# Moving work of the two bit-linear stages from VectorE and ScalarE to GpSimd: half of the normalising, most residual adds, and a shorter split into high and low parts

## The chip, the core and the metric

The kernel runs on one core of one Trainium2 chip. The metric is the device time of one execution in microseconds (us); the number that counts is the median of several runs. Engines are named as the profile names them: PE is TensorE, DVE is VectorE, ACT is ScalarE, POOL is GpSimd, SP is SyncE, which here only issues DMAs.

## The reference, cut to what matters

The network is a chain of six stages on 4 x 1024 rows of 256 features. The fourth and the sixth stage are the same "bit-linear" layer, and only they are touched:

```python
def _L1_ffn_ref(x, weight, ln_gamma, ln_beta):
    mu, var = mean(x), var(x)                              # over the 256 features
    xn = (x - mu) * rsqrt(var + 1e-3) * ln_gamma + ln_beta
    beta = mean(abs(weight))
    w_q = clip(round(weight / (beta + 1e-5)), -1, 1)
    gamma = max(abs(xn))                                   # over ALL rows
    xq = clip(xn * 128 / gamma, -128 + 1e-5, 128 - 1e-5)
    return (xq @ w_q) * (gamma * beta / 128)
...
x = x + 0.5 * _L1_ffn_ref(layernorm(x), ...)               # stage 4
x = x + _L1_attn_ref(layernorm(x), ...)                    # stage 5
x = x + 0.5 * _L1_ffn_ref(layernorm(x), ...)               # stage 6
```

The largest value over all rows splits the layer into two halves: nothing can be scaled before every row has been normalised.

## The kernel before, in words

The rows stay in SBUF for the whole kernel as `G.x`: 32 tiles of 128 rows by 256 features. `bit_phase` works on eight blocks (`NC`) of four tiles (`CT`). Each engine has its own program written out in order, and semaphores tie them together: `wait_ge` holds an engine, and everything queued behind on it, until a count is reached. A stage begins and ends with a barrier of all engines.

**First half.** For each block DVE normalises the four tiles (L1127, one `tensor_scalar` per tile with two per-row operands, written to `xn`, two buffers). PE transposes them into PSUM (`psT`, two buffers, L1197), ACT brings them to SBUF as `xT` with gain and bias (L1075), and DVE takes the largest absolute value (L1119, `largest(i-1)`, which stands behind `normalise(i)` on DVE). `normalise(i)` waits until the transposes of block i-2 are done. In between DVE sums the weights (L1106); GpSimd adds that over the partitions (L1061, `partition_all_reduce` to `wall`); DVE then makes the ternary weights (L1110 to L1114). At the end GpSimd takes the largest over the partitions (L1063, `gall`), and DVE works out `osc` and `gi` (L1138 to L1141).

**Second half.** ACT scales a block in place by `gi` (L1080), DVE clips it in place (L1145), ACT writes the fp16 high part `xhi` (L1085), DVE the fp16 rest `xlo` (L1152). PE multiplies both with the weights into `psY` (16 matmuls, L1208, two buffers). DVE adds the scaled result to the rows (L1158). In stage 4 DVE also takes the moments of the new rows for the next layernorm (L1166, L1172); in stage 6 SP sends each block out (L1054). `xhi`, `xlo` and `psY` have two buffers each, so block i waits for the matmuls (or the add) of block i-2.

Of the kernel before, what the change touches and what calls it, by code (L numbers as in the profile page):

```python
# [1004 lines left out]
def bit_phase(nc, G, A, r, out=None):  # L1005
# [3 lines left out]
    with ExitStack() as ctx:  # L1009
# [22 lines left out]
        xT = sb("xT", [P, NC, KD, CW])  # L1032
        xhi = sb("xhi", [P, 2, KD, CW], F16)
# [4 lines left out]
        s = sems(nc, ctx, f"bit{r}", "w_in gb_in eps sd norm var sd2 scl wsum wall quant xn xT xTev tmax max1 gmax gdve "  # L1038
                 "scaled xq xhi xlo Y out sums stat stored")
        block = ctx.enter_context(nc.Block())  # L1040

        @block.sync
        def _(sp):
# [6 lines left out]
            if last_phase:  # L1050
                rows = out.rearrange("b (t p) d -> p (b t) d", p=P)
                for i in range(NC):
                    sp.wait_ge(s["out"], ONE + i + 1)
                    sp.dma_start(rows[:, i * CT:(i + 1) * CT, :],  # L1054
                                 G.x[:, i * CT:(i + 1) * CT, :]).then_inc(s["stored"], 16)
# [3 lines left out]
        def _(pool):  # L1059
            pool.wait_ge(s["wsum"], ONE + 1)  # L1060
            nc.gpsimd.partition_all_reduce(wall[:, :], wsum[:, :], P, bass.bass_isa.ReduceOp.add).then_inc(s["wall"], 1)  # L1061
            pool.wait_ge(s["max1"], ONE + 1)
            nc.gpsimd.partition_all_reduce(gall[:, :], pmax[:, :], P, bass.bass_isa.ReduceOp.max).then_inc(s["gmax"], 1)  # L1063

        @block.scalar
        def _(act):
# [10 lines left out]
            act.wait_ge(s["gdve"], ONE + 4)  # L1077
            for i in range(NC + 1):
                if i < NC:
                    nc.scalar.activation(xT[:, i, :, :], xT[:, i, :, :], ACT.Copy, scale=gi[:, :]).then_inc(s["scaled"], 1)  # L1080
                if i >= 1:
                    act.wait_ge(s["xq"], ONE + i)
                    if i >= 3:
                        act.wait_ge(s["Y"], ONE + i - 2)
                    nc.scalar.activation(xhi[:, (i - 1) % 2, :, :], xT[:, i - 1, :, :], ACT.Copy).then_inc(s["xhi"], 1)  # L1085

        @block.vector
        def _(dve):
# [33 lines left out]
            for i in range(NC):  # L1122
                if i >= 2:
                    dve.wait_ge(s["xT"], ONE + (i - 1) * KD)
                for t in range(CT):
                    g = i * CT + t
                    nc.vector.tensor_scalar(xn[:, i % 2, t, :], G.x[:, g, :], G.mv[:, g, 0:1], scl[:, g:g + 1],  # L1127
                                            ALU.subtract, ALU.mult).then_inc(s["xn"], 1)
# [9 lines left out]
            step(dve, nc.vector.tensor_tensor(osc[:, :], gall[:, :], wall[:, :], ALU.mult), g)  # L1138
            step(dve, nc.vector.tensor_scalar(osc[:, :], osc[:, :], 0.5 / QB, None, ALU.mult), g)
# [1252 lines left out]
```

## Time and profile before

| | us |
|---|---|
| median of 3 runs (2425.19 to 2429.5) | 2425.92 |
| the profiled execution | 2436.6 |
| its span (first to last instruction) | 2434.7 |
| stage 4, first half (949.5 to 979.7 of the span) | 30.2 |
| stage 4, second half (979.7 to 1020.6) | 40.9 |
| stage 6, first half (2370.8 to 2401.0) | 30.2 |
| stage 6, second half (2401.0 to 2429.6) | 28.6 |
| last store and end (2429.6 to 2434.7) | 5.1 |
| busy over the span: PE 83%, DVE 66%, ACT 51%, POOL 20% | |

The two touched stages are 135 us of 2434.7, and the shares over the whole span say little about them. In the second half of stage 6 DVE is busy for 24.0 of 28.6 us, PE for 18.0, ACT for 16.7 and GpSimd not at all; in the first half of stage 4 DVE has 24.2 of 30.2 us. The stages have to be read one by one, in the timeline.

### The profile page before, as it was taken

How to read it: one execution, taken by the hardware profiler on the slowest of the kernel's cores; microseconds unless marked ns; L12 is line 12 of the kernel's file. 1: busy time of each engine (PE TensorE's matmuls, PEld its weight loads, DVE VectorE, ACT ScalarE, POOL GpSimd, SP SyncE). 2: the span in 40 equal slices, each digit the busy share in tenths (PEclk: the TensorE clock that was granted, in tenths of full speed). 3: DMA queues.
4: the chain of work that ended last, by engine and by line, in shares of the span. 5: the costliest groups of instructions: out<-in, count | busy, mean ns of one | idle time of the engine just before them, and what ended most of it. 6: DMA issues, size and time to landing. Idle time of an engine off the chain costs nothing. (4 is left out here: it accounts for less than half of the span.)

```text
span 2434.7 us, 74675 instructions
## 1 busy us (share of the span) xinstructions
PE 2030.2 (83%) x32204; PEld 1285.8 (53%) x32280; DVE 1617.5 (66%) x2553; ACT 1234.3 (51%) x1862; POOL 493.8 (20%) x794
## 2 busy tenths in 40 slices
PE   3986887888887796497773999999999999999975
PEld 2654555556455564354673555555555555555544
DVE  6775354453533677774353888888888888888847
ACT  3761221223212575322330677767777777777754
POOL 0002000000000000000001554444543454435410
PEclk7998999998989898698886899999999999999996
DMA  3001000000000000133237555544555455545412
GB/s 106 1 1 43 3 1 19 2 19 3 1 19 2 1 1 5 25 122 114 105 149 244 148 139 135 137 123 118 135 136 136 131 138 134 132 125 135 110 31 74
DMA packets 273793, 195.13 MB, mean 80 GB/s; under 512 B 206744, under 2 KB 260310, under 8 KB 273210
## 3 DMA queue, kind: packets, MB, share of 16 engines
q1 hardware_dynamic: 262586, 139.27, 22.5%
q0 software_dynamic: 10496, 50.75, 5.5%
q8 instruction: 256, 4.19, 0.7%
q14 instruction: 71, 0.58, 0.1%
q10 hardware_dynamic: 384, 0.33, 0.1%
HBM read 91.69 MB, written 93.88 MB: 76 GB/s over the span
## 5 line engine op out<-in xcount | busy, mean ns | idle before, releaser
L2020 DVE TENSOR_REDUCE a1c_nm<-a1c_S 128x1 f32<-128x1024 f32 x512 | 609.6, 1218 | 98.9 <-PE a1c_S L2105 98.3
L1960 ACT ACTIVATE a1c_PT<-a1c_ST 128x1024 f32<-128x1024 f32 x499 | 510.3, 1023 | 57.5 <-PE a1c_ST L2105 54.7
L1975 ACT ACTIVATE a1c_Pb<-a1c_S,a1c_nm 128x192 f32<-128x192 f32 (+1 forms) x512 | 212.9, 416 | 217.7 <-DVE a1c_nm L2020 216.7
L1904 POOL TENSOR_TENSOR a1c_lt<-a1c_lt 128x256 f32<-128x256 f32 (+5 forms) x448 | 254.7, 568 | 35.4
L2010 DVE COPY a1c_PbT<-a1c_T 96x512 f32<-96x512 f32 x256 | 175.7, 686 | 96.1 <-PE a1c_T L2137 93.7
L2105 PE MATMUL a1c_S<-a1c_KR,a1c_Q 54*32 54x512 f16 (+13 forms) x2816 | 180.7, 316 | 19.7 <-DMA a1c_Gx<-a_bias 18.3
L2105 PE MATMUL a1c_ST<-a1c_Q,a1c_KR 57*128 57x256 f16 (+2 forms) x1066 | 175.0, 284 | 22.3 <-ACT a1c_PT L1960 21.5
L2105 PE MATMUL a1c_S<-a1c_KL,a1c_Q 54*32 54x512 f16 (+11 forms) x3136 | 191.8, 323 | 0.6 <-ACT a1c_Pb L1975 0.3
L2105 PE MATMUL a1c_S<-a1c_Gx,ident 64*32 64x96 f32 (+2 forms) x4352 | 184.8, 240 | 0.0
L1896 POOL DMA_DIRECT2D a_band<-a1c_Pb x128 | 71.4, 558 | 495.6 <-ACT a1c_Pb L1975 495.3
L2137 PE MATMUL a1c_T<-ident,a1c_Pb 128*96 128x128 f32 x1024 | 168.1, 288 | 0.8 <-DVE a1c_mhl L2034 0.8
L2105 PE MATMUL a1c_ST<-a1c_Q,a1c_KL 57*128 57x128 f16 (+1 forms) x932 | 148.9, 265 | 19.2 <-ACT a1c_PT L1960 16.8
L1061 POOL PARTITION_ALL_REDUCE b_wall<-b_wsum x2 | 0.8, 406 | 799.1 <-DVE b_wsum L1106 799.1
L593 ACT ACTIVATE a_PT<-a_R 128x2048 f32<-128x2048 f32 x40 | 75.1, 1878 | 148.9 <-PE a_R L894 126.8
L2137 PEld LDWEIGHTS a1c_T<-ident,a1c_Pb 128*96 128x96 f32 x1024 | 101.9, 128 | 87.8 <-issue 55.4
L318 DVE TENSOR_TENSOR f_hlo<-f_h,f_hhi 128x512 f16<-128x512 f32 x128 | 88.0, 688 | 69.2 <-ACT f_hhi L236 69.2
L2105 PEld LDWEIGHTS a1c_S<-a1c_Gx,ident 64*32 64x32 f32 x4352 | 125.4, 109 | 13.6 <-issue 0.7
L231 ACT ACTIVATE f_h<-f_psH,b,a 128x512 f32<-128x512 f32 x128 | 99.3, 776 | 59.9 <-PE f_psH L342 58.4
L2105 PE MATMUL a1c_PV<-a1c_PT,a1c_VU 128*17 128x512 f32 (+3 forms) x1280 | 127.5, 470 | 0.0
L2105 PE MATMUL a1c_PV<-a1c_PT,a1c_VL 128*17 128x512 f32 (+3 forms) x1280 | 126.8, 468 | 0.2 <-issue 0.2
L1595 DVE TENSOR_TENSOR a1b_G<-a1b_k,a1b_G 128x512 f32<-128x512 f32 x96 | 65.7, 691 | 88.7 <-PE a1b_k L1601 49.5
L648 DVE TENSOR_REDUCE a_mt<-a_R 128x16 f32<-128x2048 f32 x32 | 73.4, 2293 | 75.0 <-PE a_R L835 75.0
(344 smaller groups left out, 4138.4 us busy)
## 6 DMA issues: line engine op xcount, KB each, us to landing
a_band<-a1c_Pb POOLq DMA_DIRECT2D x128, 384.0 KB, 3.3
a_bias<-a1b_G SPq DMA_DIRECT2D x32, 768.0 KB, 8.1
a1c_Gx<-a_bias SPq DMA_DIRECT2D x128, 192.0 KB, 4.3
a1c_Dt<-a_band SPq DMA_DIRECT2D x128, 126.0 KB, 3.7
a1c_Q<-a_qk SPq DMA_DIRECT2D x192, 64.0 KB
a1c_Vw<-a_values SPq DMA_DIRECT2D x64, 102.0 KB, 2.8
a1c_KL<-a_qk SPq DMA_DIRECT2D x96, 64.0 KB
a1c_KR<-a_qk SPq DMA_DIRECT2D x90, 64.0 KB
```

Source lines behind the costliest of these rows:

```text
L231: nc.scalar.activation(h[:, n % NB, :], psH[:, n % NB, :], ACT.Gelu, bias=G.b1[:, m:m + 1], scale=G.a1[:, m:m + 1]).then_inc(s["h"], 1)
L318: nc.vector.tensor_tensor(hlo[:, n % NB, :], h[:, n % NB, :], hhi[:, n % NB, :], ALU.subtract).then_inc(s["hlo"], 1)
L593: nc.scalar.activation(PT[:, n % 2, :, :], R[:, :, :], ACT.Exp, scale=0.25).then_inc(s["sexp"], 1)
L648: nc.vector.tensor_reduce(dst, src, AX.X, ALU.max, negate=True).then_inc(s["smax"], 1)
L1896: pool.dma_start(PW[b * S + I * P:b * S + I * P + P, 4 * hq:4 * hq + 4, :], Pb[:, at:at + 4, :]).then_inc(s[f"pw{g // 4 % 2}"], 16)
L1904: add = lambda o, x, y: nc.gpsimd.tensor_tensor(o, x, y, ALU.add)
L1960: nc.scalar.activation(PT[:, q % 8, :, :], place(q), ACT.Exp).then_inc(s["exp"], 1)
L1975: nc.scalar.activation(Pb[:, band_slot(I, c), w0:w1], SP[:, t % 2, I * P - 32 + w0:I * P - 32 + w1], ACT.Exp, bias=nm[:, t // 16 % 2, col: ...
L2010: nc.vector.tensor_copy(PbT[:, e % RING, :], T[0:BW, :]).then_inc(s["Tb_ev"], 1)
L2020: nc.vector.tensor_reduce(nm[:, t // 16 % 2, col:col + 1], SP[:, t % 2, :], AX.X, ALU.max, negate=True).then_inc(s["max"], 1)
L2105: return nc.tensor.matmul(out, w, x, start=start, stop=stop, skip_group_check=True)
L2137: ins = nc.tensor.transpose(T[0:BW, at:at + P], Pb[:, band_slot(I, c), BW * ch:BW * ch + BW], G.ident[:, :])
```

## The change

- First half: a helper `normalise` deals the tiles out. DVE takes tiles 0 and 2 of each block, GpSimd tiles 1 and 3, with a semaphore of its own (`xnp`). PE waits for both. GpSimd's all-reduce of the weight sum stands behind its tiles of block 1 and ahead of those of block 2.
- `gi` is worked out first; `osc` follows after the first block's low part.
- Second half: ACT writes `xhi` straight from `xT` with the scale `gi`. DVE scales and cuts at the upper bound into a new buffer `x1`, and cuts at the lower bound as it subtracts `xhi` (`scalar_tensor_tensor`). The step that scaled `xT` in place is gone.
- The scaled product goes from PSUM to a new buffer `ys` on ACT, and GpSimd adds it to the rows, for blocks 0 to 6. DVE does block 7 in one instruction, as before.

```diff
+        x1 = sb("x1", [P, 2, KD, CW])
+        ys = sb("ys", [P, 2, CT, D])
...
+        def normalise(eng, on, i, k, done):
+            for t in range(k, CT, 2):
+                g = i * CT + t
+                on.tensor_scalar(xn[:, i % 2, t, :], G.x[:, g, :], G.mv[:, g, 0:1], scl[:, g:g + 1],
+                                 ALU.subtract, ALU.mult).then_inc(done, 1)
...
         def _(pool):
+            pool.wait_ge(s["scl"], ONE + 2)
+            for i in range(NC):
+                if i >= 2:
+                    pool.wait_ge(s["xT"], ONE + (i - 1) * KD)
+                normalise(pool, nc.gpsimd, i, 1, s["xnp"])
+                if i == 1:
+                    pool.wait_ge(s["wsum"], ONE + 1)
+                    nc.gpsimd.partition_all_reduce(wall[:, :], wsum[:, :], P, bass.bass_isa.ReduceOp.add).then_inc(s["wall"], 1)
             pool.wait_ge(s["max1"], ONE + 1)
             nc.gpsimd.partition_all_reduce(gall[:, :], pmax[:, :], P, bass.bass_isa.ReduceOp.max).then_inc(s["gmax"], 1)
+            for i in range(NC - 1):
+                rows = G.x[:, i * CT:(i + 1) * CT, :]
+                pool.wait_ge(s["ys"], ONE + i + 1)
+                nc.gpsimd.tensor_tensor(rows, ys[:, i % 2, :, :], rows, ALU.add).then_inc(s["out"], 1)
...
-            act.wait_ge(s["gdve"], ONE + 4)
+            act.wait_ge(s["gdve"], ONE + 2)
             for i in range(NC + 1):
                 if i < NC:
-                    nc.scalar.activation(xT[:, i, :, :], xT[:, i, :, :], ACT.Copy, scale=gi[:, :]).then_inc(s["scaled"], 1)
-                if i >= 1:
-                    act.wait_ge(s["xq"], ONE + i)
-                    if i >= 3:
-                        act.wait_ge(s["Y"], ONE + i - 2)
-                    nc.scalar.activation(xhi[:, (i - 1) % 2, :, :], xT[:, i - 1, :, :], ACT.Copy).then_inc(s["xhi"], 1)
+                    if i >= 2:
+                        act.wait_ge(s["Y"], ONE + i - 1)
+                    nc.scalar.activation(xhi[:, i % 2, :, :], xT[:, i, :, :], ACT.Copy, scale=gi[:, :]).then_inc(s["xhi"], 1)
+                if i == 1:
+                    act.wait_ge(s["gdve"], ONE + 4)
+                if i >= 2:
+                    act.wait_ge(s["Y"], ONE + i - 1)
+                    if i >= 4:
+                        act.wait_ge(s["out"], ONE + i - 3)
+                    nc.scalar.activation(ys[:, i % 2, :, :], psY[:, i % 2, :, :], ACT.Copy, scale=osc[:, :]).then_inc(s["ys"], 1)
...
             def clip(i):
-                dve.wait_ge(s["scaled"], ONE + i + 1)
-                nc.vector.tensor_scalar(xT[:, i, :, :], xT[:, i, :, :], CLIP, -CLIP, ALU.min,
-                                        ALU.max).then_inc(s["xq"], 1)
+                if i >= 2:
+                    dve.wait_ge(s["xlo"], ONE + i - 1)
+                nc.vector.tensor_scalar(x1[:, i % 2, :, :], xT[:, i, :, :], gi[:, :], CLIP, ALU.mult,
+                                        ALU.min).then_inc(s["xq"], 1)
...
-                nc.vector.tensor_tensor(xlo[:, i % 2, :, :], xT[:, i, :, :], xhi[:, i % 2, :, :],
-                                        ALU.subtract).then_inc(s["xlo"], 1)
+                nc.vector.scalar_tensor_tensor(xlo[:, i % 2, :, :], x1[:, i % 2, :, :], -CLIP, xhi[:, i % 2, :, :],
+                                               ALU.max, ALU.subtract).then_inc(s["xlo"], 1)
...
             for i in range(NC):
-                pe.wait_ge(s["xn"], ONE + i * CT + CT)
+                pe.wait_ge(s["xn"], ONE + i * 2 + 2)
+                pe.wait_ge(s["xnp"], ONE + i * 2 + 2)
...
                 if i >= 2:
-                    pe.wait_ge(s["out"], ONE + i - 1)
+                    pe.wait_ge(s["ys"], ONE + i - 1)
```

The order of GpSimd's instructions in stage 4 before (L1058 begins its part; an ISA row without a tile is the change of library, one with a tile is an all-reduce):

```order
L1058 UNCONDITIONAL_BRANCH
L1061 ISA
L1061 ISA b_wall<-b_wsum 128x1
L1063 ISA b_gall<-b_pmax 128x1
L1009 UNCONDITIONAL_BRANCH
```

And the same place after the change (L1053 is the helper `normalise`, L1081 and L1083 the all-reduces, L1087 the adds):

```order
L1072 UNCONDITIONAL_BRANCH
L1053 ISA
L1053 TENSOR_SCALAR b_xn<-x,mv,b_scl 128x256 x4
L1081 ISA
L1081 ISA b_wall<-b_wsum 128x1
L1053 ISA
L1053 TENSOR_SCALAR b_xn<-x,mv,b_scl 128x256 x12
L1083 ISA
L1083 ISA b_gall<-b_pmax 128x1
L1087 ISA
L1087 TENSOR_TENSOR x<-b_ys,x 128x1024 x7
L1009 UNCONDITIONAL_BRANCH
```

Where there was one change of library there are five in stage 4; in stage 6 there are four, since the first one is missing there (the library is still loaded from stage 5).

DVE in the second half of stage 4 before, from `gi` on:

```order
L1141 TENSOR_SCALAR b_gi<-b_gi 128x1
L1145 TENSOR_SCALAR b_xT<-b_xT 128x1024 x2
L1152 TENSOR_TENSOR b_xlo<-b_xT,b_xhi 128x1024
L1145 TENSOR_SCALAR b_xT<-b_xT 128x1024
L1152 TENSOR_TENSOR b_xlo<-b_xT,b_xhi 128x1024
L1158 SCALAR_TENSOR_TENSOR x<-b_psY,b_osc,x 128x1024
L1145 TENSOR_SCALAR b_xT<-b_xT 128x1024
L1152 TENSOR_TENSOR b_xlo<-b_xT,b_xhi 128x1024
L1158 SCALAR_TENSOR_TENSOR x<-b_psY,b_osc,x 128x1024
L1166 BN_STATS b_sums<-x 128x6 x4
```

And after the change:

```order
L1164 TENSOR_SCALAR b_gi<-b_gi 128x1
L1169 TENSOR_SCALAR b_x<-b_xT,b_gi 128x1024
L1177 SCALAR_TENSOR_TENSOR b_xlo<-b_x,b_xhi 128x1024
L1181 TENSOR_TENSOR b_osc<-b_gall,b_wall 128x1
L1182 TENSOR_SCALAR b_osc<-b_osc 128x1
L1169 TENSOR_SCALAR b_x<-b_xT,b_gi 128x1024
L1177 SCALAR_TENSOR_TENSOR b_xlo<-b_x,b_xhi 128x1024
L1169 TENSOR_SCALAR b_x<-b_xT,b_gi 128x1024
L1177 SCALAR_TENSOR_TENSOR b_xlo<-b_x,b_xhi 128x1024
L1169 TENSOR_SCALAR b_x<-b_xT,b_gi 128x1024
L1177 SCALAR_TENSOR_TENSOR b_xlo<-b_x,b_xhi 128x1024
L1195 BN_STATS b_sums<-x 128x6 x4
```

The residual has left DVE's loop, and the low part of a block stands right behind its own cut, one block earlier in the loop than before.

## Rows read from the trace of the kernel before

**Rows 1.** Timeline: start us, us, engine, line, op [idle before <-releaser]; stage 4 opens.

```profile
953.04 2.67 DVE L1127 TENSOR_SCALAR b_xn<-x,mv,b_scl 128x256 f32<-128x256 f32 x8
...
956.45 0.41 POOL L1061 PARTITION_ALL_REDUCE b_wall<-b_wsum  x1 [755.63 <-DVE b_wsum L1106]
...
959.86 1.09 PE L1197 MATMUL b_psT<-ident,b_xn 128*128 128x128 f32 x8 [2.00 <-DVE b_xn L1127]
...
978.32 0.16 DVE L1135 TENSOR_REDUCE b_pmax<-b_tmax 128x1 f32<-128x8 f32 x1
...
979.75 2.19 ACT L1080 ACTIVATE b_xT<-b_xT,b_gi 128x1024 f32<-128x1024 f32 x2 [2.72 <-DVE b_gi L1141]
```

**Rows 2.** Timeline, stage 6, first half: where blocks 2 and 4 pass.

```profile
2381.18 1.97 PE L1197 MATMUL b_psT<-ident,b_xn 128*128 128x128 f32 x8 [1.71 <-DVE b_xn L1127]
...
2390.19 1.97 PE L1197 MATMUL b_psT<-ident,b_xn 128*128 128x128 f32 x8 [0.45 <-DVE b_xn L1127]
...
2393.01 1.22 DVE L1119 TENSOR_REDUCE b_tmax<-b_xT 128x1 f32<-128x1024 f32 x1
2394.14 1.37 DVE L1127 TENSOR_SCALAR b_xn<-x,mv,b_scl 128x256 f32<-128x256 f32 x4
...
2395.57 1.97 PE L1197 MATMUL b_psT<-ident,b_xn 128*128 128x128 f32 x8 [0.45 <-DVE b_xn L1127]
```

**Rows 3.** The chain that ended last, stage 6: start us, us, what.

```profile
2374.37 2.67 DVE b_xn L1127 x8
...
2401.08 2.19 ACT b_xT L1080 x2
...
2404.24 1.24 DVE b_xlo L1152
...
2405.61 3.58 PE b_psY L1208 x16
...
2426.36 1.94 PE b_psY L1208 x16
...
2428.32 1.28 DVE x L1158
```

**Rows 4.** Timeline of DVE, second half of stage 4, one block, and its last instruction.

```profile
995.36 1.25 DVE L1158 SCALAR_TENSOR_TENSOR x<-b_psY,b_osc,x 128x1024 f32<-128x1024 f32 x1
996.53 1.39 DVE L1166 BATCH_NORM_STATS2 b_sums<-x 128x6 f32<-128x256 f32 x4
...
999.85 1.25 DVE L1158 SCALAR_TENSOR_TENSOR x<-b_psY,b_osc,x 128x1024 f32<-128x1024 f32 x1
...
1020.17 0.38 DVE L1172 BATCH_NORM_AGGREGATE mv<-b_sums 128x2 f32<-128x6 f32 x4
```

**Rows 5.** Line L101, the kernel's first change of library: duration min/median/max ns, start us.

```profile
L101 POOLq MODIFY_POOL_CONFIG  x2: 11/11/11, 1.3 to 1.3; - x2
L101 POOL TENSOR_SCALAR_AFFINE_SELECT ident<-ident x1: 1239/1239/1239, 8.4 to 8.4; 128x128 f32<-128x128 f32 x1
```

**Rows 6.** Line L1061, the changes of library in both stages, same columns.

```profile
L1061 POOLq MODIFY_POOL_CONFIG  x4: 11/11/11, 949.7 to 2371.0; - x4
```

**Rows 7.** GpSimd's two-input instructions by form: busy us, mean ns.

```profile
L1904 POOL TENSOR_TENSOR a1c_lt<-a1c_lt 128x256 f32<-128x256 f32 x128 | 93.2, 728 | 10.0
L1920 POOL TENSOR_TENSOR a1c_VL<-a1c_VU,a_rvd 128x512 f32<-128x512 f32 x16 | 19.2, 1198 | 22.1 <-DMA a1c_VU<-a_values 21.8
L1926 POOL TENSOR_TENSOR x<-x,a1c_bp 128x2048 f32<-128x2048 f32 x4 | 18.2, 4547 | 0.1
```

**Rows 8.** Line L618, the same normalising on DVE at 183 to 198 us, GpSimd busy.

```profile
L618 DVE TENSOR_SCALAR a_xn<-x,mv,rstd x8: 1256/1316/5331, 183.6 to 196.1; 128x256 f32<-128x256 f32 x8
```

**Rows 9.** DVE instructions by form: busy us, mean ns.

```profile
L1127 DVE TENSOR_SCALAR b_xn<-x,mv,b_scl 128x256 f32<-128x256 f32 x64 | 21.8, 407 | 0.1
L1145 DVE TENSOR_SCALAR b_xT<-b_xT 128x1024 f32<-128x1024 f32 x16 | 11.0, 684 | 3.1 <-ACT b_xT L1080 3.1
L1152 DVE TENSOR_TENSOR b_xlo<-b_xT,b_xhi 128x1024 f16<-128x1024 f32 x16 | 19.5, 1219 | 0.8 <-ACT b_xhi L1085 0.8
```

More of the change, by code:

```diff
@@ L1037, in bit_phase, with wait_out @@
         psY = ps("psY", [P, 2, CT, D])
-        s = sems(nc, ctx, f"bit{r}", "w_in gb_in eps sd norm var sd2 scl wsum wall quant xn xT xTev tmax max1 gmax gdve "
-                 "scaled xq xhi xlo Y out sums stat stored")
+        s = sems(nc, ctx, f"bit{r}", "w_in gb_in eps sd norm var sd2 scl wsum wall quant xn xnp xT xTev tmax max1 gmax gdve "
+                 "xq xhi xlo Y ys out out_v sums stat stored")
         block = ctx.enter_context(nc.Block())
+        def wait_out(eng, i):
+            if i < NC - 1:
+                eng.wait_ge(s["out"], ONE + i + 1)
+            else:
+                eng.wait_ge(s["out_v"], ONE + 1)
+        def normalise(eng, on, i, k, done):
[3 more added lines that the diff above has]
+                                 ALU.subtract, ALU.mult).then_inc(done, 1)
         @block.sync
@@ L1124, in _ @@
                     dve.wait_ge(s["xT"], ONE + (i - 1) * KD)
[L1125 to L1128, printed above, removed]
+                normalise(dve, nc.vector, i, 0, s["xn"])
                 if i in (1, 3):
@@ L1151, in low_part, with out_scale, residual @@
                     dve.wait_ge(s["Y"], ONE + i - 1)
-                nc.vector.tensor_tensor(xlo[:, i % 2, :, :], xT[:, i, :, :], xhi[:, i % 2, :, :],
-                                        ALU.subtract).then_inc(s["xlo"], 1)
-            def residual(i):
-                rows = G.x[:, i * CT:(i + 1) * CT, :]
-                dve.wait_ge(s["Y"], ONE + i + 1)
-                nc.vector.scalar_tensor_tensor(rows, psY[:, i % 2, :, :], osc[:, :], rows, ALU.mult,
-                                               ALU.add).then_inc(s["out"], 1)
+                nc.vector.scalar_tensor_tensor(xlo[:, i % 2, :, :], x1[:, i % 2, :, :], -CLIP, xhi[:, i % 2, :, :],
+                                               ALU.max, ALU.subtract).then_inc(s["xlo"], 1)
+            def out_scale():
+                step(dve, nc.vector.tensor_tensor(osc[:, :], gall[:, :], wall[:, :], ALU.mult), g)
+                step(dve, nc.vector.tensor_scalar(osc[:, :], osc[:, :], 0.5 / QB, None, ALU.mult), g)
+            def residual():
+                rows = G.x[:, (NC - 1) * CT:, :]
+                dve.wait_ge(s["Y"], ONE + NC)
+                nc.vector.scalar_tensor_tensor(rows, psY[:, (NC - 1) % 2, :, :], osc[:, :], rows, ALU.mult,
+                                               ALU.add).then_inc(s["out_v"], 1)
             def moments(i):
-                dve.wait_ge(s["out"], ONE + i + 1)
+                wait_out(dve, i)
                 if i >= 1:
```

16 lines of the change are left out of this document (7 added, 9 removed).

## The prediction, made before the changed kernel was run

> **What bounds the kernel now.** The two touched stages are 135 us of 2434.7, so busy shares over the span say nothing; I read the timeline stage by stage, then the chain, then the costs of single lines. In the first half DVE is nearly always busy, yet the length is set by a ring. The transposes of one block start at 2390.19, ACT is done 2.8 later, DVE takes the largest (1.2, from 2393.01), then normalises the block after next (1.37), whose transposes start at 2395.57 [rows 2]. So two blocks cost 5.38. In the second half DVE sets the pace: cut 0.6, low part 1.15 and residual 1.2 make 2.93 per block in stage 6, and with the moments one block takes 4.49 in stage 4 (995.36 to 999.85 [rows 4]). The chain of stage 6 runs through `xlo`, the matmuls and the residual [rows 3]. GpSimd is idle there but for two all-reduces [rows 1].
>
> **First part of the change: GpSimd's order, with changes of library.** Every time GpSimd goes from all-reduce to ordinary arithmetic or back, the new order has a change of library. Its price is in the trace once, in the open: it is issued at 1.3 and the next instruction starts at 8.4, 7.1 us later, waiting for nothing else [rows 5]. A second row bounds it: issued at 949.7, the all-reduce starts at 956.45, just behind the weight sum it waits for, so the change was done within 6.7 [rows 6, 1]. Before, that one was hidden behind the start of the stage. I take 6.5, with 5.5 and 7.1 as ends, since one row allows less than 6.7; zero is a rival below. The skill says something here, and it does not carry the sum: "GPSIMD Engine Reference" of the Trainium skill, section 2.1 Instruction dispatch, has the first call after such a change pay about 6 us (5.95) for loading code. The 7.1 agrees in kind; by 5.95 the sum below would be some 4 us smaller.
>
> GpSimd's `tensor_scalar` on 128x256 has no row. Two inputs of that size take 0.73 [rows 7], DVE takes 0.34 to 0.41 for it [rows 2, 9]; I take 0.5, nearer the lower end because it reads one input, with 0.35 and 0.73 as ends.
>
> Stage 4: change issued at 949.7, done 956.2; four tiles (blocks 0 and 1), 958.2; change to all-reduce, 964.7; all-reduce 0.4, 965.1; change back, 971.6; two tiles of block 2, 972.6. The transposes of block 2 wait for that; they started at 959.86 [rows 1]: **+12.7**. DVE, PE and ACT all stand behind it, since DVE's next step needs that block. Stage 6: no change at the start; `scl` is ready at 2374.37 [rows 3], GpSimd gets the tiles once DVE's first four are through (see below), 2375.7; then 2377.7, 2384.2, 2384.6, 2391.1, 2392.1, against 2381.18 [rows 2]: **+10.9**.
>
> From there to the largest value took 18.6 (959.86 to 978.48 [rows 1]). After: the ring is shorter by half a normalising, 5.38 - 0.67 = 4.7; twice that for blocks 4 and 6, 2.0 until block 7, 2.8 + 1.2 + 0.2 for its end, 15.7: **-2.9** in each stage. The last change of library before the all-reduce of the largest is issued when block 7 is normalised, 5.3 to 6.0 ahead of the largest value by the same steps, so 0.5 to 1.2 of it stands out: **+0.7**. `gi` comes two small steps earlier: **-0.4**. The change ahead of the adds is hidden: the first add comes 8.9 after `gi`. Sum at `gi`: stage 4 12.7 - 2.9 + 0.7 - 0.4 = **+10.1**, stage 6 10.9 - 2.9 + 0.7 - 0.4 = **+8.3**.
>
> **Second part: the adds beside DVE.** A row shows that these two engines do not simply run side by side. DVE's `tensor_scalar` on 128x256 takes 0.41 [rows 9], but at 183 to 198, with GpSimd busy without a pause, eight of them took 1.26 to 5.33, median 1.32 [rows 8]. Each one waited for a whole GpSimd instruction. The new cut is such a `tensor_scalar` (SBUF to SBUF), so it excludes the add. For the low part, which reads two SBUF tiles, no row shows either; its cost from this lies between nothing and full exclusion. I take full exclusion, as the nearest row for an SBUF-to-SBUF step of DVE has it. Beside that stands a rule: "SBUF — State Buffer" of the Trainium skill, section Who interferes with whom, says that a DVE instruction with two SBUF inputs, or in its two-port mode, and a GpSimd instruction that reads SBUF lock each other out for a whole instruction. It speaks against this change; no run here shows the two-input half of it.
>
> GpSimd's add on 128x1024: 1.2 for 512 and 4.55 for 2048 elements [rows 7], 2.3 in between. Cut and low part keep 0.65 + 1.2 = 1.85 [rows 9, 3]. One block then costs 1.85 + 2.3 = **4.15** of the shared resource, against 2.93 in stage 6 and 4.49 in stage 4 before.
>
> From `gi` to the first add: high part 1.1, low part 1.2 (in place of the four steps to 2405.5, a gain of 2.1), 16 matmuls 3.5 at the 1.2 GHz that PE has at this point (3.58 against 1.94 later at 2.4 [rows 3]), high part of block 2 1.1, its low part and the next cut 1.85: 8.9 with the hand-overs. Stage 6: 8.9, four times 4.15, then add, low part, add, add = 2.3 + 1.2 + 2.3 + 2.3: 33.6. Before, 2401.04 to 2429.60 = 28.6 [rows 3]: **+5.0**. The residual of block 7 on DVE and its matmuls finish earlier than the last add, so they cost nothing; if the adds were quick, they would be the end. Stage 4: seven adds 16.2; the moments (1.4, one input) run beside an add and let a second add pass, so only about four cut-and-low pairs stand between them, 7.5; with 8.9 the last add ends at 32.6; low part 7, four rounds of moments and the residual follow on DVE, 9.4: 42.0. Before, 979.71 to 1020.55 = 40.8 [rows 1, 4]: **+1.2**. ACT's new evacuation (1.1) and high part (1.1) make 2.2 per block, hidden under 4.15; uncovered it would set 2.2. Stores follow the adds on SP, and the tail of 5.1 stays.
>
> **Sum**: 10.1 + 8.3 + 5.0 + 1.2 = 24.6, **+25 us**. The profiled execution would go from 2436.6 to about 2461; the median of the runs is 10.7 lower than the profiled one, 2425.9 + 25 = **2451**. Laid out in this way with the old steps, the ends of both stages come within 0.3 us of the trace's.
>
> **Rivals.** (1) *Reload paid, but only the cut and the normalising exclude GpSimd, the low part does not.* Then a block costs 0.65 + 2.3 = 3.0 in stage 6, and stage 4 falls back to DVE's own 3.5: 8.5 less, +16, 2442. For it: no row has a two-input step blocked. Against: none has it free.
> (2) *Reload paid, no exclusion at all.* GpSimd's 2.3 per block is the pace of stage 6, 3.5 on DVE that of stage 4; the second halves gain 4 and 8, and the first halves lose the 18 less 2 for waits: about +4, 2430. Against: rows 8.
> (3) *The other side: changing the library costs nothing on the path*, for instance because a library seen once stays. The place is GpSimd's tiles of block 2. First halves then gain 3.9 each (three rings 2.0, the start 1.5, `gi` 0.4), and with no exclusion the second halves gain 8 and 4: -20, 2406. With exclusion the normalising takes turns too, which leaves 1.7 in each first half: against the 6.2 of the second halves +3, 2429, or, with the cut alone excluding, second halves of 6.2 - 8.5 and -6, 2420. The sign turns, without exclusion, where a change costs 5.8; with the cut alone excluded, at 3.3; with full exclusion it does not turn. For it: nothing says that a library loaded before must be loaded again. Against: rows 5 and the fact that the order has a change each time.
> (4) *Changing costs more than 7.1 each, or the first instruction after one is slow* (the first after rows 5 took 1.24): each further us costs 7 in all, +30 or more.
>
> **How the numbers follow.** Forecast 0.56, its own range 2446 to 2460: changes of 5.5 to 7.1 give +20 to +30, tiles of 0.35 to 0.73 -3 to +4. Rival 1 0.17, rival 2 0.09, rival 3 0.12 (0.05 without exclusion, 0.02 with the cut alone, 0.05 in full), rival 4 0.06. The range **2428 to 2462** takes in the forecast, rival 1, most of rival 2 and the full-exclusion case of rival 3, and leaves out some 0.17. A measurement here can tell about 0.2%, 4.9 us, from no change. Faster by more: the two cases of rival 3, 0.07. Within: half of rival 2 and the case of +3, 0.10. Slower: 0.83.
>
> **What would show it.** Right: in both stages GpSimd's first tile of block 2 starts about 6.5 after the all-reduce of the weight sum, with nothing it waits for, and PE's transposes of block 2 at about 973 and 2392; `gi` at about 990 and 2409; cuts and low parts of DVE that last 3 us or start only when an add ends; adds 4.15 apart in stage 6. Wrong: block 2's transposes before 962, adds of 2.3 beside low parts of 1.2 (rivals 1 and 2), or a second half of stage 6 shorter than 28. If PE stayed at 1.2 GHz through the second half, a block would need 3.5 there, still hidden under 4.15. What would make it wrong altogether is a library change that runs ahead while GpSimd waits.

## The result

The changed kernel takes **2471.4 us** (median of four runs, 2467.4 to 2475.6) against 2427.7 for the kernel before (2425.2 to 2431.5): a ratio of 1.0179, with an interval of 1.0155 to 1.0203. It is slower by 43.7 us, where 25 were forecast, and lies 9 us above the top of the range. The profiled execution took 2469.6 us, its span is 2467.9.

The profile of after says where. I cut both stages as the prediction did: the first half runs from the stage's first instruction on DVE to the first one that uses `gi`, the second to the last instruction that writes `x`, the tail to the end of the span.

| us | stages 1 to 3 | 4, first | 4, second | stage 5 | 6, first | 6, second | tail | the two stages |
|---|---|---|---|---|---|---|---|---|
| before | 949.5 | 30.2 | 40.8 | 1350.3 | 30.2 | 28.5 | 5.1 | 134.9 |
| after | 942.1 | 43.2 | 43.8 | 1353.7 | 43.8 | 34.7 | 6.6 | 172.1 |
| forecast | | 40.3 | 42.0 | | 38.5 | 33.6 | 5.1 | 159.5 |

The two stages that were changed grew by 37.2: 26.6 in the first halves, 9.2 in the second, 1.5 in the tail.

**First halves.** GpSimd in stage 6, from its timeline (start us, us, engine, line, op, idle before and what ended it):

```profile
2386.33 5.03 POOL L1053 TENSOR_SCALAR b_xn<-x,mv,b_scl 128x256 f32<-128x256 f32 x4 [39.97 <-DVE b_scl L1127]
2397.17 0.40 POOL L1081 PARTITION_ALL_REDUCE b_wall<-b_wsum  x1 [5.82 <-issue]
2405.03 14.82 POOL L1053 TENSOR_SCALAR b_xn<-x,mv,b_scl 128x256 f32<-128x256 f32 x12 [7.46 <-issue]
2425.76 0.38 POOL L1083 PARTITION_ALL_REDUCE b_gall<-b_pmax  x1 [5.91 <-issue]
2435.11 2.44 POOL L1087 TENSOR_TENSOR x<-b_ys,x 128x1024 f32<-128x1024 f32 x1 [8.97 <-ACT b_ys L1113]
```

Every passage from the tiles to an all-reduce or back has 5.8 to 7.5 us of "issue" ahead of it: GpSimd waits for nothing that the profile shows. These are the changes of library. GpSimd waits for nothing else until `gi`: from the stage's start 3.6 to its first tile, then 5.0 + 5.8 + 0.4 + 7.5 + 14.8 + 5.9 + 0.4, and 0.4 on DVE for `gi` make the 43.8, and in stage 4 the same steps make the 43.2. So GpSimd's own work is the path through the whole first half, with 19.9 of tiles and 19.2 of changes (stage 6). The profile's chain, below, goes by the other engines' steps there and has 1.6 of issue left over behind the largest value; GpSimd's steps leave nothing over. The second thing to see is the length of the tiles: four of them 5.03. The line by itself (duration min/median/max in ns, first and last start) has both engines side by side:

```profile
L1053 DVE TENSOR_SCALAR b_xn<-x,mv,b_scl x32: 401/407/636, 945.6 to 2418.7; 128x256 f32<-128x256 f32 x32
L1053 POOL TENSOR_SCALAR b_xn<-x,mv,b_scl x32: 1208/1216/1408, 945.7 to 2418.6; 128x256 f32<-128x256 f32 x32
```

The same instruction takes 0.41 on DVE and 1.22 on GpSimd; the forecast had 0.5. DVE's stay short even where a tile of GpSimd runs beside them (24 of the 32 do so, the longest took 0.64), so here neither engine waits out the other's instruction. Everybody stands behind block 2, as the timeline of stage 6 shows, with PE's transposes of blocks 1 and 2 and DVE's first largest value after them:

```profile
2391.50 1.94 PE L1228 MATMUL b_psT<-ident,b_xn 128*128 128x128 f32 x8 [0.46 <-POOL b_xn L1053]
...
2407.58 1.94 PE L1228 MATMUL b_psT<-ident,b_xn 128*128 128x128 f32 x8 [14.14 <-issue]
...
2410.37 1.22 DVE L1147 TENSOR_REDUCE b_tmax<-b_xT 128x1 f32<-128x1024 f32 x1 [10.92 <-ACT b_xT L1099]
```

In [rows 2] those transposes come 10.35 after the stage's start at 2370.8, here 24.9 after 2382.7.

In stage 4 the all-reduces have the same 5.67 and 5.84 ahead of them and the tiles of block 2 6.95, but ahead of the first tiles, at 945.69, no time is lost to a change:

```profile
945.69 5.03 POOL L1053 TENSOR_SCALAR b_xn<-x,mv,b_scl 128x256 f32<-128x256 f32 x4 [745.27 <-DVE b_scl L1127]
956.39 0.40 POOL L1081 PARTITION_ALL_REDUCE b_wall<-b_wsum  x1 [5.67 <-issue]
963.74 14.89 POOL L1053 TENSOR_SCALAR b_xn<-x,mv,b_scl 128x256 f32<-128x256 f32 x12 [6.95 <-issue]
984.48 0.38 POOL L1083 PARTITION_ALL_REDUCE b_gall<-b_pmax  x1 [5.84 <-issue]
```

**Second halves.** DVE in stage 6, five steps of its timeline:

```profile
2434.10 1.23 DVE L1177 SCALAR_TENSOR_TENSOR b_xlo<-b_x,b_xhi 128x1024 f16<-128x1024 f32 x1 [2.09 <-ACT b_xhi L1106]
2435.24 2.85 DVE L1169 TENSOR_SCALAR b_x<-b_xT,b_gi 128x1024 f32<-128x1024 f32 x1
2438.13 3.25 DVE L1177 SCALAR_TENSOR_TENSOR b_xlo<-b_x,b_xhi 128x1024 f16<-128x1024 f32 x1
2441.30 2.83 DVE L1169 TENSOR_SCALAR b_x<-b_xT,b_gi 128x1024 f32<-128x1024 f32 x1
2444.16 1.23 DVE L1177 SCALAR_TENSOR_TENSOR b_xlo<-b_x,b_xhi 128x1024 f16<-128x1024 f32 x1
```

A cut takes 0.75 when it is alone and 2.85 beside an add, a low part 1.23 and 3.25. The excess is 2.0 to 2.1, just under the 2.35 of an add: the instruction waits out the rest of the add that is running. The adds wait in the same way, with 2.34 at the least and 3.33 at the most:

```profile
L1087 POOL TENSOR_TENSOR x<-b_ys,x x14: 2344/2458/3328, 993.6 to 2458.3; 128x1024 f32<-128x1024 f32 x14
```

The chain that ended last runs through these steps (start us, us, what):

```profile
2424.16 1.60 issue
2425.76 0.39 POOL b_gall L1083
...
2429.19 3.59 PE b_psY L1239 x16
...
2438.13 3.26 DVE b_xlo L1177
2441.39 0.05 issue
2441.43 3.47 PE b_psY L1239 x16
...
2456.23 1.24 DVE b_xlo L1177
2457.46 0.05 issue
2457.51 2.49 PE b_psY L1239 x16
2460.00 0.03 issue
2460.02 1.28 DVE x L1187
```

It shows both kinds of price: 1.6 of issue between the largest value and its all-reduce, and low parts of 3.26. It shows a third thing as well. The matmuls that follow a long low part, after 4.1 in which PE stood idle, take 3.47 for a block, against 1.94 in [rows 3]. The granted clock there is 0.53, so nearly all of it ran at the lower level of 1.2 GHz, where before's block of 1.94 had 1.00 (2.4 GHz):

```profile
2441.40:2445.00 3.60, 3.46 (x16) 2.17 (x16) 3.56 (x2) 0.07 (x1) 2.18 (x1) 0.53 0.54 182
2426.60:2461.30 34.70, 21.48 (x128) 15.07 (x128) 29.18 (x19) 15.94 (x15) 18.99 (x7) 0.73 0.27 92
```

The columns are the stretch, us, the busy times of PE, weight loads, DVE, ACT and GpSimd, then clock, DMA share and GB/s. Over the whole second half, the second line, the clock is 0.73 of full speed, where before's second half of stage 6 had 0.82.

### The profile page after: what moved, and what is told of

Read it like the earlier page. It is cut to its first block and busy times, and to the rows that moved or that the text cites. A ratio compares the mean times of both kernels' runs of the same rounds, so it can differ in the third digit from the quotient of the medians.

```text
span 2467.9 us, 74775 instructions
## 1 busy us (share of the span) xinstructions
PE 2045.2 (83%) x32280; PEld 1284.4 (52%) x32280; DVE 1615.6 (65%) x2507; ACT 1232.1 (50%) x1860; POOL 568.0 (23%) x840
## 5 line engine op out<-in xcount | busy, mean ns | idle before, releaser
L1935 POOL TENSOR_TENSOR a1c_lt<-a1c_lt 128x256 f32<-128x256 f32 (+5 forms) x448 | 253.9, 567 | 35.4
L1053 POOL TENSOR_SCALAR b_xn<-x,mv,b_scl 128x256 f32<-128x256 f32 x32 | 39.7, 1250 | 799.7 <-DVE b_scl L1127 785.2
```

Of the source, the lines that this page charges most:

```text
L1935: add = lambda o, x, y: nc.gpsimd.tensor_tensor(o, x, y, ALU.add)
```

## The experiments

The theory after the result: the first halves pay for changes of library and for GpSimd tiles of 1.22, the second halves for DVE and GpSimd shutting each other out in cut and low part. Against it stood that one half's loss might come from the other (a clock, a late `x`), that changes cost less than they seem and only the slow tiles count, and that low parts are long for another reason than the adds. The runs are read by the table of stages, since a profile shows a stage to some tenths of a us while whole runs of one kernel differ by 5 and more. All stages in us; medians where a kernel was timed in rounds, with their ratio to before on the same chip.

| | 4, first | 4, second | 6, first | 6, second | tail | the two stages | against before |
|---|---|---|---|---|---|---|---|
| before | 30.2 | 40.8 | 30.2 | 28.5 | 5.1 | 134.9 | 1 |
| after | 43.2 | 43.8 | 43.8 | 34.7 | 6.6 | 172.1 | 1.0179 |
| adds alone | 29.9 | 43.6 | 29.7 | 34.4 | 7.0 | 144.6 | 1.0047 |
| tiles alone | 43.6 | 40.8 | 43.6 | 28.5 | 5.7 | 162.2 | 1.0119 |
| all-reduces last | 30.1 | 46.8 | 30.9 | 37.5 | 5.7 | 151.0 | 1.0103 |
| one tile | 38.1 | 47.4 | 38.1 | 36.0 | 5.7 | 165.3 | one run |
| two changes, in before | 36.4 | 41.4 | 36.3 | 28.5 | 5.7 | 148.3 | one run |
| scratch adds, in before | 30.2 | 52.1 | 30.2 | 41.2 | 5.7 | 159.4 | one run |
| scratch memsets, in before | 30.2 | 44.4 | 30.2 | 35.4 | 5.7 | 146.0 | one run |
| short split | 29.9 | 40.4 | 29.9 | 26.9 | 5.1 | 132.1 | 0.9996 |
| short split, a tile on ACT | 28.0 | 40.4 | 28.0 | 26.8 | 5.1 | 128.3 | 0.9972 |

### The two parts apart

**Adds alone** is the changed kernel with its first half as before: DVE normalises every tile, GpSimd has only the all-reduces there.

```diff
-            for t in range(k, CT, 2):
+            for t in range(CT):
...
-            pool.wait_ge(s["scl"], ONE + 2)
-            for i in range(NC):
-                ...
-                normalise(pool, nc.gpsimd, i, 1, s["xnp"])
...
+            pool.wait_ge(s["wsum"], ONE + 1)
+            nc.gpsimd.partition_all_reduce(wall[:, :], wsum[:, :], P, bass.bass_isa.ReduceOp.add).then_inc(s["wall"], 1)
```

> First half of both stages as in the kernel before (DVE normalises every tile), second half as in the changed kernel (GpSimd adds, ACT's scaled copy, short split). Theory (library changes and GpSimd's slow tiles cost the first halves 26 us, mutual exclusion of DVE and GpSimd the second halves 9 and the tail 1.5): first halves back to 30 us each, second halves 43 to 44 and 34 to 35, total 9 to 12 above before. Rival (what was lost in the second halves comes from their late start, with PE at 1.2 GHz after the long idle time): the second halves too fall back to 41 or less and 29 or less, total within 3 of before or faster.

Measured: 2446.55 against 2430.4, ratio 1.0047 (1.0022 to 1.0072). The first halves are those of before to 0.6, the second ones those of after to 0.3.

**Tiles alone** is the kernel before with the changed first half:

```diff
+                normalise(pool, nc.gpsimd, i, 1, s["xnp"])
+                if i == 1:
...
...
-                for t in range(CT):
-                    nc.vector.tensor_scalar(xn[:, i % 2, t, :], ...)
+                normalise(dve, nc.vector, i, 0, s["xn"])
```

> First half as in the changed kernel (GpSimd normalises tiles 1 and 3), second half as before (DVE cuts and adds everything). Theory: first halves 43 to 44 us each in place of 30, second halves 41 and 28.6 as before, total 25 to 29 above before. Rival (the parts are not independent, the adds' library change is what makes the first half long): first halves under 38, total under +16.

Measured: 2459.01, ratio 1.0119 (1.008 to 1.0158), first halves 43.6, second halves as before. Over before the two stages grew by 9.7 and by 27.3; together that is 37.0, and the whole change has 37.2. So the parts add up, and neither half's loss comes from the other. The adds alone also carry the longer tail (7.0): the last add on GpSimd and DVE's residual end 0.2 us apart there (2439.7 and 2439.9), so that two stores are left for the end.

### How much of the first halves is library, how much the tiles

**All-reduces last** is the changed kernel with both all-reduces behind GpSimd's last tile, so that one change of library is left in the first half; the ternary weights follow behind DVE's first low part.

```diff
                 normalise(pool, nc.gpsimd, i, 1, s["xnp"])
-                if i == 1:
-                    pool.wait_ge(s["wsum"], ONE + 1)
-                    nc.gpsimd.partition_all_reduce(wall[:, :], ...)
+            pool.wait_ge(s["wsum"], ONE + 1)
+            nc.gpsimd.partition_all_reduce(wall[:, :], ...)
             pool.wait_ge(s["max1"], ONE + 1)
...
-                if i in (1, 3):
-                    quantise(i // 2)
+                if i == 1:
+                    quantise(0)
...
                 if i == 0:
+                    quantise(1)
                     out_scale()
```

> The changed kernel, but the all-reduce of the weight sum stands next to that of the largest value at the end of GpSimd's first half, and the ternary weights are made after the first block's low part. That removes two changes of library from the middle of each first half and puts 1.75 us of DVE work and 0.4 of all-reduce later. Theory (each change costs 5.7 to 7.4 on the path): first halves 43 to about 31, the second ones up to 2 longer, total 18 to 24 below the changed kernel. Rival (GpSimd's tiles of 1.22 us are what makes the first half long, the changes are mostly hidden): at most 8 below the changed kernel.

Measured: 2456.34, ratio 1.0103 (1.0066 to 1.0139). The two stages are 21.2 below after: the first halves fall from 43.2 and 43.8 to 30.1 and 30.9, and the second ones, with the weights in them now, grow by 3.0 and 2.7. GpSimd in stage 6:

```profile
2381.81 19.74 POOL L1053 TENSOR_SCALAR b_xn<-x,mv,b_scl 128x256 f32<-128x256 f32 x16 [40.00 <-DVE b_scl L1126]
2407.91 0.40 POOL L1080 PARTITION_ALL_REDUCE b_wall<-b_wsum  x1 [6.35 <-issue]
2408.23 0.44 POOL L1082 PARTITION_ALL_REDUCE b_gall<-b_pmax  x1
```

Sixteen tiles take 19.74, two per block 2.47, and the transposes of one block follow those of the last in 2.44. The chain that ended last runs through them:

```profile
2381.81 1.39 POOL b_xn L1053
2383.21 18.35 POOL b_xn L1053 x15
...
2401.80 6.11 issue
2407.91 0.40 POOL b_wall L1080
```

So GpSimd's tiles and one change of library are the whole path of this first half, and that it is as long as before's is a coincidence. From block 2's transposes to the largest value it takes 16.4 in place of 18.6, by the shorter normalising; but those transposes start 0.9 later, and 1.6 to 2.4 of the change stand out behind the largest value. Halving DVE's normalising gained nothing, because GpSimd's tiles of 1.22 became the pace.

**One tile** leaves one tile of four to GpSimd and three to DVE:

```diff
-            for t in range(k, CT, 2):
+            for t in ((3,) if k else (0, 1, 2)):
```

> The changed kernel with GpSimd normalising one tile per block (3) in place of two, DVE three. Theory (a GpSimd tile of 1.22 us ahead of each change of library lengthens the path: two tiles fewer before the first change, one fewer before block 2's transposes): each first half 3.5 shorter than in the changed kernel, about 40, less 0.5 for DVE's longer ring: 40 to 41. Rival (the tiles are hidden, only the changes count): 43 to 44 as before.

Measured: first halves of 38.1, 5.1 and 5.7 below after. More than expected, and the trace says why. Three tiles instead of six stand ahead of block 2, 3 x 1.22 = 3.7, and its transposes come 3.4 and 4.1 earlier. From there to the largest value it takes 0.6 less. And GpSimd is done early enough that its all-reduce comes 0.5 after the largest value in place of 1.6, so that the profile has it waiting for that value again:

```profile
987.34 0.38 POOL L1083 PARTITION_ALL_REDUCE b_gall<-b_pmax  x1 [5.91 <-DVE b_pmax L1160]
```

The second halves brought a surprise. Their code is that of after, and stage 4's took 47.4, not 43.8 (one execution of each). Low parts of stage 4 on DVE in both kernels, after first (busy us, mean ns):

```profile
L1177 DVE SCALAR_TENSOR_TENSOR b_xlo<-b_x,b_xhi 128x1024 f16<-128x1024 f32 x8 | 11.8, 1478 | 2.6 <-ACT b_xhi L1106 2.4
```

```profile
L1177 DVE SCALAR_TENSOR_TENSOR b_xlo<-b_x,b_xhi 128x1024 f16<-128x1024 f32 x8 | 15.9, 1983 | 2.8 <-ACT b_xhi L1106 2.6
```

4.1 us more in which low parts wait for adds: three of the eight are long in place of one. That this depends on where the steps happen to fall is my reading; what is measured is that the length of such a stage differs by some us for the same code.

### What one change of library costs

**Two changes** puts a GpSimd instruction of no use to the result (128x1 elements) between the largest value and its all-reduce, in the kernel before:

```diff
             pool.wait_ge(s["max1"], ONE + 1)
+            nc.gpsimd.tensor_scalar(tiny[:, :], pmax[:, :], 0.5, None, ALU.mult).then_inc(s["tiny"], 1)
+            pool.wait_ge(s["tiny"], ONE + 1)
             nc.gpsimd.partition_all_reduce(gall[:, :], ...)
```

> The kernel before, with one GpSimd multiplication of 128x1 between the largest value over the blocks and the all-reduce of it, so that a change of library and the change back stand on the path and nothing else is added. Theory: about 7.2 and 5.8, each first half 13 longer (43), total +26. Rival (a change of library is cheap when no data moves besides, or a library that was loaded once is kept): under +4 in all.

Measured: +6.2 and +6.1 in the first halves, half of what was expected, and so a miss that tells more than a hit. Stage 4:

```profile
956.49 0.40 POOL L1062 PARTITION_ALL_REDUCE b_wall<-b_wsum  x1 [755.71 <-DVE b_wsum L1109]
978.63 0.27 POOL L1064 TENSOR_SCALAR b_tiny<-b_pmax 128x1 f32<-128x1 f32 x1 [21.73 <-DVE b_pmax L1138]
984.79 0.38 POOL L1066 PARTITION_ALL_REDUCE b_gall<-b_pmax  x1 [5.89 <-issue]
```

The change toward arithmetic was asked for just behind the first all-reduce, which ends at 956.90, and ran while GpSimd waited for the largest value; the small instruction starts as soon as that is there. Here is the change's own row (min/median/max ns, first and last start us):

```profile
L1064 POOLq MODIFY_POOL_CONFIG  x4: 83/83/83, 956.9 to 2390.3; - x4
```

Only the change back is in the open, 5.89 and in stage 6 5.77. So a change doesn't begin when the wait ahead of its instruction ends but when the instruction before it is done. It is hidden by any wait as long as itself, and in the changed kernel nothing like it stands ahead of the tiles of block 2: there is 5.8 + 7.5 with no wait between.

A change can also cost nothing at all. In before, the first instruction behind the change at L101 starts 7.1 later [rows 5]; in after it starts at once (1.46 to 1.52):

```profile
L101 POOLq MODIFY_POOL_CONFIG  x2: 11/11/11, 1.4 to 1.5; - x2
L101 POOL TENSOR_SCALAR_AFFINE_SELECT ident<-ident x1: 292/292/292, 1.5 to 1.5; 128x128 f32<-128x128 f32 x1
```

The eleven profiles divide without exception: at once in the five kernels whose last change is the one toward arithmetic for adds, 6.8 to 7.7 later in the six whose last change is the one toward an all-reduce. That reads as a library that stays loaded from one execution to the next, and as a change that is free when its library is already there. Stages 1 to 3 show no gain from it (941 to 950 us in the five, 938 to 950 in the six).

### Who shuts whom out

Both kernels are the one before, with work for GpSimd on a scratch tile beside its second halves; it is extra work, and so only the length of DVE's instructions and of the halves is read. **Scratch adds** has two memsets and then seven adds of 128x1024 in each stage, **scratch memsets** ten memsets of 128x2560, each about as long as an add (2.2 to 2.7) but writing only.

```diff
+            nc.gpsimd.memset(scr[:, 0, :], 0.0)
+            nc.gpsimd.memset(scr[:, 1, :], 0.0)
+            for i in range(7):
+                nc.gpsimd.tensor_tensor(scr[:, 2, 0:1024], scr[:, 0, 0:1024], scr[:, 1, 0:1024], ALU.add)
```

```diff
+            for i in range(10):
+                nc.gpsimd.memset(scr[:, i % 3, :], 0.0)
```

> The kernel before, with seven GpSimd adds of 128x1024 on tiles of their own, which nobody waits for, beside the second half of each stage. Theory (DVE and GpSimd exclude each other for a whole instruction if DVE works SBUF to SBUF in its fast form, or reads two SBUF tiles): while the adds run, the cut and also the low part last up to 3 us in place of 0.68 and 1.22, the residual (one input from PSUM) stays at 1.28; the second halves grow by 5 to 10 each. Rival 1 (only the cut is excluded): low parts stay at 1.22, growth 3 to 5. Rival 2 (the long instructions of the changed kernel came from its data flow): nothing grows by more than 0.5.

> The same with ten GpSimd memsets of 128x2560 (about 2.3 us each), which read nothing. Theory: the cut waits for whole memsets, the low part (two reads, one write) does not and stays at 1.22. Rival (any GpSimd instruction excludes any SBUF-only DVE instruction): low parts last up to 3 us as in the run with adds.

DVE beside the adds: cut, low part, residual (min/median/max ns).

```profile
L1152 DVE TENSOR_SCALAR b_xT<-b_xT x16: 670/1644/2827, 972.5 to 2441.9; 128x1024 f32<-128x1024 f32 x16
```

```profile
L1159 DVE TENSOR_TENSOR b_xlo<-b_xT,b_xhi x16: 1201/1224/3371, 976.5 to 2444.8; 128x1024 f16<-128x1024 f32 x16
```

```profile
L1165 DVE SCALAR_TENSOR_TENSOR x<-b_psY,b_osc,x x16: 1244/1272/1285, 981.5 to 2448.0; 128x1024 f32<-128x1024 f32 x16
```

And beside the memsets, the first two of them:

```profile
L1149 DVE TENSOR_SCALAR b_xT<-b_xT x16: 670/1540/2757, 978.5 to 2436.8; 128x1024 f32<-128x1024 f32 x16
```

```profile
L1156 DVE TENSOR_TENSOR b_xlo<-b_xT,b_xhi x16: 1203/1206/1218, 981.8 to 2439.7; 128x1024 f16<-128x1024 f32 x16
```

Here the steps of DVE share no tile with GpSimd's work and wait for none of its results, and they are as long as in after. So it is the engine beside them, not the kernel's own order. The cut, which in one read and one write goes from SBUF to SBUF (0.67 for 1024 elements), is held up by both kinds; the low part, which reads two tiles of SBUF, by the reading add alone (up to 3.37) and never by the memset (1.22 at most, though ten of the sixteen run beside one); the residual, one of whose two tiles is in PSUM, by neither (1.29 at most). "SBUF — State Buffer" of the Trainium skill, section Who interferes with whom, has just this: two SBUF inputs against a GpSimd instruction that reads SBUF, and the two-port mode against any. The two traces agree with the first, and with the second if the cut runs in that mode, which no row names. That section has the one engine blocked for the other's whole instruction; the cuts and low parts show this, the normalising of the first half doesn't, with 0.23 lost at most.

The second halves grew by 11.3 and 12.7 beside the adds, where 5 to 10 were expected; two memsets of 2.3 ahead of the adds are part of it, and how the rest adds up I did not follow.

### Is there a gain in it at all

**Short split** keeps what is good in the new second half (ACT writes the high part straight from `xT`, DVE clips and scales in one) and gives GpSimd nothing; DVE adds every residual between cut and low part.

```diff
-            for i in range(NC - 1):
-                pool.wait_ge(s["ys"], ONE + i + 1)
-                nc.gpsimd.tensor_tensor(rows, ys[:, i % 2, :, :], rows, ALU.add).then_inc(s["out"], 1)
...
                     clip(i)
+                if 2 <= i <= NC + 1:
+                    residual(i - 2)
+                if i < NC:
                     low_part(i)
```

> No work on GpSimd beyond the two all-reduces: ACT writes the high part straight from xT with the scale, DVE scales and cuts into x1 and takes the low part, and DVE adds every block from PSUM. Theory: DVE's pace per block stays 3.0 and 4.5, the start of each second half is 2.1 us shorter and gi comes 0.4 earlier, cuts with a pointer cost 0.07 each more: 4 us faster than before. Rival (DVE is bound everywhere, the start is paid back at the end): within 1 us of before. Rival (the ring through the high part's wait on the matmuls binds with two buffers): up to 5 slower.

Measured: 2428.54 against 2430.4, ratio 0.9996 (0.9979 to 1.0012), the two stages 2.8 shorter, 1.6 of it at the second half of stage 6 and 0.4 at that of stage 4. No difference that a run can tell. DVE is the pace of these halves, and the new cut costs it as much as the old one or more; here is the new one, to be read against the 684 of [rows 9]:

```profile
L1148 DVE TENSOR_SCALAR b_x<-b_xT,b_gi x16: 734/746/753, 968.0 to 2413.1; 128x1024 f32<-128x1024 f32 x16
```

**Short split with a tile on ACT** then tries the idea of the first half with an engine that has neither a library to change nor a quarrel with DVE: ACT normalises the fourth tile of each block, `x * scl + nb` with `nb` = -mean x `scl` from one small instruction of DVE.

```diff
+            def own_tile(i):
+                nc.scalar.activation(xn[:, i % 2, CT - 1, :], G.x[:, g, :], ACT.Identity, bias=nb[:, g:g + 1],
+                                     scale=scl[:, g:g + 1]).then_inc(s["xna"], 1)
...
-            for t in range(CT):
+            for t in range(CT - 1):
```

> The short split without GpSimd, and ACT normalises tile 3 of each block (an activation with scale and bias per row, right behind its evacuations), DVE three tiles. Theory (the first half is set by the ring transposes, evacuation, largest value, normalising on DVE): each ring of two blocks 0.34 shorter, first halves about 28.7 in place of 29.9, total 5 below the kernel before (0.2%). Rival (ACT's extra 0.5 per block delays the evacuations): first halves 30 or more, total as with the short split alone.

Measured: 2425.61 (12 runs) against 2435.2 (16) on the same chip, ratio 0.9972 (0.9952 to 0.9992). It beats the kernel before by 0.3%, by more than the runs' uncertainty though not by much, and the changed kernel by far. The first halves are 2.2 shorter. ACT takes 0.59 for a tile and DVE's own stay at 0.41, so neither is held up by the other:

```profile
L1084 ACT ACTIVATE b_xn<-x,b_nb,b_scl x16: 585/591/600, 950.7 to 2385.6; 128x256 f32<-128x256 f32 x16
```

```profile
L1050 DVE TENSOR_SCALAR b_xn<-x,mv,b_scl x48: 402/405/409, 950.6 to 2387.5; 128x256 f32<-128x256 f32 x48
```

## Why the prediction was right or wrong

**The mechanisms held.** Both of the forecast's are in the traces: a change of library in the open on the path to block 2, once each way, and full exclusion of cut and low part. For the low part the exclusion was a choice between two ends that no row decided, and it came true. It was taken for the normalising too, and there it failed: DVE's tiles beside GpSimd's took 0.41 with 0.64 at most. The 1.26 to 5.33 of [rows 8] were measured beside other GpSimd instructions, memsets and selections of 0.9 to 1.2; what makes the difference stays open. Rival 1 (low part free) falls by low parts of 3.25 in after and 3.37 beside scratch adds, rival 2 with it. Rival 3 (changes free) falls by 5.8 and 7.5 of issue and by the 21.2 that come back when the all-reduces go last. "A library change that runs ahead while GpSimd waits", named as what would make it wrong altogether, does exist (two changes in before, one of them hidden). Rival 4 had the range in which the time fell (+30 or more), for another reason: the first instruction after a change took 1.41 at most, and the changes themselves are near the forecast's. The sum itself had let two changes run ahead in this way, the one before the largest value and the one before the adds. The hidden change didn't overturn the forecast, because ahead of block 2 there is no wait to hide in.

**The size did not.** The two stages grew by 37.2, not 24.6:

- *The tile on GpSimd, 0.5 with ends 0.35 and 0.73: measured 1.22.* This is the step that failed. It was bounded from above by an add of the same size [rows 7] on the thought that one input is cheaper than two. But this `tensor_scalar` takes two more operands, a mean and a scale for each row, and no row of GpSimd had that form; whether these are what makes it slow, no run tells. Six tiles ahead of block 2 make 6 x 0.72 = 4.3 in each stage, 8.6 in all. The instruction stood in [rows 9] on DVE alone, and a bound above would have had to come from rows further off. It also turned the path around: the forecast let the ring of PE, ACT and DVE set the pace behind block 2, and in the trace GpSimd goes from tile to tile without a wait and sets it.
- *Change of library, 6.5 each.* 5.8 toward the all-reduce and 7.5 toward arithmetic in stage 6: 13.3 for 13.0, a good term. The 5.95 of "GPSIMD Engine Reference" of the Trainium skill (section 2.1 Instruction dispatch) is met toward the all-reduce and exceeded by up to 1.5 the other way. In stage 4 the first of three (ending at 956.2 in the forecast) did not stand out: the tiles start 3.6 after the stage's start, in step with `scl`. That took off 3.1. The library that GpSimd used last, 745 us earlier, was one of ordinary arithmetic, so that there was probably nothing to load. The two ways the kernel starts, shown under the experiment with two changes, support this.
- *Wait of 1.3 for DVE's first tiles in stage 6*: not there. Tiles on GpSimd and DVE started within 0.1 of each other and ran side by side, -1.3. The whole for block 2 is then 14.5 in stage 6 (10.9 forecast) and 13.9 in stage 4 (12.7).
- *Ring shorter by 2.9*: 16.6 from block 2's transposes to the largest value against 18.6 before, so 2.0; +0.9 in each stage. The blocks follow each other in 2.4 to 2.5, which is GpSimd's two tiles.
- *Last change before the largest value, 0.7*: 1.6 in the chain, +0.9 in each. It is asked for when GpSimd's last tile is done, and that comes later by the slow tiles: the same error again. With one tile per block it was 0.5.
- *Second half of stage 6, 33.6*: 34.7. The first add came 8.6 after `gi` (8.9). From there to the end of the last add it was 25.5 (24.7 forecast), of which GpSimd is busy 19.0 and waits 6.6 for ACT and, through it, for PE and the low part. Matmuls of 3.5 at 1.2 GHz were to be hidden under the 4.15 of a block; here they stand in the chain behind a low part of 3.26. Then the residual of block 7, which was to be done earlier, ends 0.6 behind the last add, its matmuls having taken 2.5 where they take 1.94 at full clock.
- *Second half of stage 4, 42.0*: 43.8. Given 43.6 to 47.4 for the same code in other kernels, this isn't a number that could be had closer.
- *The tail stays 5.1*: 6.6. Since add 6 and residual 7 end within 0.7 us of each other, their stores go out together. In adds alone they end 0.2 apart and the tail is 7.0; in the nine other kernels they end 2.1 or more apart, and it is 5.1 to 5.7.

First halves +8.2, second halves +2.9, tail +1.5: 12.6 more than the sum. The price of the tile makes 12.2 of the first halves' (8.6, 1.8 and 1.8 in the items above), and what was forecast and didn't come, the first change in stage 4 and the wait in stage 6, took 4.4 off it. With 1.22 ahead of block 2 alone, the sum would have been 33.

**What is left.** 37.2 in the two stages and 43.7 between the medians leave 6.5 us in stages whose code is the same. The profile of before is a long execution of its kernel (2436.6 at a median of 2427.7), with 949.5 in stages 1 to 3 and 1350.3 in stage 5. In the eleven profiles stages 1 to 3 range over 938 to 950, though nothing ahead of them differs, and stage 5 over 1350 to 1359, with 1354 to 1356 in the four kernels with the residual adds on GpSimd and 1350 to 1359 in the others. So I see no sign that the change lengthens them. On two other chips the medians of before were 2430.4 and 2435.2, and against these the changed kernel would be 36 to 41 slower. That fits the 37.2, but one median against one of another chip isn't a comparison, and the 6.5 stays open.

## What to carry to other kernels

A move of work to GpSimd is priced in three parts, and the instruction's own time is the least certain: find the very form (its scalars too) in a trace before trusting a bound from another form. Then write down GpSimd's order and mark each place where library and arithmetic instructions alternate; a place cost 5.6 to 7.5 us here unless a wait of that length stood right before it, so all-reduces belong together or at such a wait. Then add up GpSimd's own order from end to end: once it is longer than the ring of the others, it is the path, and taking work off DVE gains nothing. And an engine that is "idle" doesn't run beside DVE for free. Beside adds and memsets DVE's cuts were held up, beside adds its low parts too, while its residuals from PSUM and its moments kept their length; beside GpSimd's normalising tiles its own lost 0.23 at most. Which pair is held up has to be read from rows of that pair.

## What the runs showed of the hardware that was not expected

- A GpSimd `tensor_scalar` with two operands per row takes 1.22 us on 128x256, against 0.73 for a two-input add of that size [rows 7], 0.41 on DVE and 0.59 for the same work on ACT.
- A change of library is paid at every passage from one to the other, for one loaded before as well: over all runs 5.6 to 6.4 in the open toward an all-reduce, 6.7 to 7.5 toward arithmetic. Where the library is already there it costs nothing that shows (0.06 at the start of five kernels, against 6.8 to 7.7 in six). It starts behind the instruction before, not behind the wait, and so two of them cost 6.1 where 13 were expected.
- A GpSimd instruction that only writes holds up the cut (2.76 for 0.67) but not the low part with its two inputs (1.22 at most); an add, which reads, holds up both. DVE's normalising and GpSimd's hardly hold each other up (0.23 and 0.28 at most). A second half of stage 4 with adds took 43.6 to 47.4 us for the same code.
- A cut with its scale from a tile takes 0.747, the one with constants 0.684, on 1024 elements.
